# Transformer block with quantized cross-attention and a 16-expert layer: the front reordered, one tile turned by a DMA

## What is computed

```
def fake_quant(x, scale, zp):
    q = clip(round(x / scale + zp), 0, 255)
    return (q - zp) * scale

# 1. attention stage: x [2,512,1024], context [2,1024,1024]
x = x + tanh(g_xattn) * matmul(fake_quant(layernorm(x)), fake_quant(context))

# 2. expert stage on xt = layernorm(x)
logits = xt @ router_w + router_b
scores = softmax(logits) + router_bias
# 2 of 4 groups by their maximum, then 2 of 16 experts in them: gate [1024,16]
for e in range(16):
    h = silu(xt @ w1[e] + b1[e]) * (xt @ w2[e] + b2[e])     # 256 wide
    y = y + gate[:, e] * (h @ w3[e] + b3[e])
z = silu(xt @ sw1 + sb1) * (xt @ sw2 + sb2) @ sw3 + sb3     # shared, 512 wide
x = x + tanh(g_ffn) * (y + z)
```

## Time and profile before

| | us |
|---|---|
| median of 3 runs | 317.7 |
| runs | 317.53 to 319.18 |
| the profiled execution | 317.24 |
| its span in the trace | 315.4 |
| PE busy | 302.6 (96%) |
| DVE busy | 206.3 (65%) |
| ACT busy | 115.0 (36%) |
| POOL busy | 13.9 (4%) |

### The profile page before, as it was taken

One profiled execution on the slowest core, in us unless ns is written; L12 is line 12 of the kernel. 1 busy time (PEld: TensorE's weight loads), 2 busy tenths in 40 slices (PEclk: granted clock), 3 DMA queues, 4 the chain that ended last, 5 costly groups with the idle time before them and its releaser, 6 DMA issues.

```text
span 315.4 us, 4716 instructions
## 1 busy us (share of the span) xinstructions
PE 302.6 (96%) x1867; PEld 153.3 (49%) x1867; DVE 206.3 (65%) x346; ACT 115.0 (36%) x129; POOL 13.9 (4%) x27
## 2 busy tenths in 40 slices
PE   4899899999999999999999999999999999999993
PEld 4653499644444446444444444444444444444441
DVE  3888999999998967776464361748564306135543
ACT  2877689589633559211108000064000000111000
POOL 2100120100002110000000000000000000000000
PEclk9999999999999999999999999999999999999999
DMA  7999908447620547105800008400000000000355
GB/s 234 410 337 321 304 12 250 150 101 214 220 66 0 108 94 72 1 2 167 301 0 2 0 0 290 178 0 0 2 0 0 2 1 1 0 2 0 134 204 202
DMA packets 43543, 34.55 MB, mean 110 GB/s; under 512 B 24060, under 2 KB 38396, under 8 KB 43516
## 3 DMA queue, kind: packets, MB, share of 16 engines
q1 hardware_dynamic: 43508, 34.20, 35.6%
q10 hardware_dynamic: 8, 0.00, 0.0%
HBM read 26.86 MB, written 4.19 MB: 98 GB/s over the span
## 4 chain that ended last, share of the span: by engine, by line
PE 60%; DVE 25%; DMA 4%; ACT 4%; issue 3%; POOL 2%; POOLq 0%; ACTq 0%; DVEq 0%; SPq 0%
PE PS L1426 26%; PE PS L1233 13%; PE PS L1447 13%; PE PS L1274 7%; DVE stats L691 6%; DVE X L778 3%; DVE areaW L755 3%; POOL lnR L399 2%; DMA areaT<-ring 2%; ACT QI L450 1%; DMA ring<-in_L_ffn_sw_dram 1%; DVE S L742 1%; DVE X L1017 1%; DVE area L738 1%; DMA X<-in_x_dram 1%
## 5 line engine op out<-in xcount | busy, mean ns | idle before, releaser
L1233 PE MATMUL PS<-areaT,areaW 128*128 128x512 f16 x288 | 62.5, 379 | 0.0
L1233 PEld LDWEIGHTS PS<-areaT,areaW 128*128 128x128 f16 x288 | 28.0, 98 | 33.7
L1274 PE MATMUL PS<-SW,areaH 128*128 128x512 f16 x192 | 41.8, 379 | 0.0
L1447 PE MATMUL PS<-areaW,areaH 128*128 128x512 f16 x192 | 41.8, 379 | 0.0
L1426 PE MATMUL PS<-areaT,area 128*128 128x512 f16 x192 | 41.6, 379 | 0.0
L1426 PE MATMUL PS<-areaT,areaW 128*128 128x512 f16 x192 | 41.6, 379 | 0.0
L635 ACT ACTIVATE SA<-PS,ecol 128x512 f32<-128x512 f32 x8 | 5.5, 689 | 93.2 <-PE PS L1426 93.2
L1105 DVE SCALAR_TENSOR_TENSOR X<-PS,gcol,X 128x1024 f32<-128x1024 f32 (+1 forms) x18 | 21.0, 1165 | 15.8 <-PE PS L1447 15.8
L1076 DVE SCALAR_TENSOR_TENSOR SA<-PS,ecol,SA 128x512 f32<-128x512 f32 x8 | 6.0, 751 | 38.2 <-ACT SA L635 38.2
L1176 PE MATMUL PS<-area,areaQ 128*128 128x512 f16 x128 | 30.0, 379 | 0.9 <-DVE areaQ L721 0.3
L1274 PEld LDWEIGHTS PS<-SW,areaH 128*128 128x128 f16 x192 | 18.8, 98 | 22.6
(11 more groups left out here) (164 smaller groups left out, 308.8 us busy)
## 6 DMA issues: line engine op xcount, KB each, us to landing
areaT<-in_ctx_dram SPq DMA_DIRECT2D x12, 512.0 KB, 8.1
ring<-in_L_ffn_sw_dram SPq DMA_DIRECT2D x12, 512.0 KB, 5.4
X<-in_x_dram SPq DMA_DIRECT2D x8, 512.0 KB, 5.9
ring<-in_L_ffn_ew_dram SPq DMA_DIRECT2D x4, 1024.0 KB, 7.2
out_dram<-X SPq DMA_DIRECT2D x7, 512.0 KB, 2.6
ring<-in_ctx_dram SPq DMA_DIRECT2D x4, 512.0 KB, 3.8
wrow<-in_L_ffn_ew_dram SPq DMA_DIRECT2D x2, 1024.0 KB, 9.6
rows<-in_L_ffn_eb_dram SPq DMA_DIRECT2D x2, 512.0 KB, 9.5
```

The lines of the kernel that those rows point to most:

```text
L1233: last = mm(PS[:, SU_BANK[half * SC + c] + w, lo:hi], SW[:, wp, 2 * c + w, k, :], XT[:, xp, k, tk], start=(k == 0 and n == 0), stop=(k == ...
L1274: last = mm(PS[:, pb + h, :], HT[:, hp, c, i * P:(i + 1) * P], SW3[:, wp, c, hs], start=(c == 0 and n == 0), stop=(c == SC - 1 and n == 2))
L1447: last = mm(PS[:, 2 * (i % 2) + h, :], HE[:, hp, c, i * P:(i + 1) * P], W3S[j][:, wp, c, hs], start=(c == 0 and n == 0), stop=(c == HC - 1 ...
```

## The change

1. SP loads context tile 0 ahead of x tile 1, x tile 2 ahead of context tile 2, and x tile 3 behind context tile 4.
2. VectorE's and ScalarE's queues of the front are written in another order. All four tiles are copied from PSUM by ScalarE (`evac_q1`). The context column sum is no longer added right behind each clamp, but later where it fits. Four of the six coefficient operations in `cf` now stand behind the first tile's statistics, and a fifth behind tile 0's coefficients.
3. TensorE's order follows; fewer idle products stand in it (14 + 32 + 14 + 30, before 14 + 32 + 14 + 18 + 10 + 26).
4. No `open_block`: the first product into a bank starts it.
5. The fourth normed tile is turned by a transposing transfer that SP issues between weight chunks 6 and 7. TensorE's two transposes and ScalarE's two copies for it are gone. `first_low` runs over the first three tiles (384 columns), then `row_sums`, then all products of the fourth tile.
6. `add_columns` of tiles 5, 6 and 7 runs on GpSimd, each ahead of the tile's attend; tile 4 stays with VectorE.
7. `token_sum` of tiles 6 and 7 and `row_terms(1)` stand behind the second half's coefficients instead of ahead of the fourth `su_gate`; the load of `SB3` stands behind the turned tokens.

The core of the diff:

```diff
@@ SP
+            for r in range(4, 7):
+                load_chunk(r)
+            sp.wait_ge(ln_hi, TB)
+            sp.wait_ge(ln_lo, TB)
+            sp.dma_start_transpose(XT[:, :, :, S - P:S].rearrange("p h k t -> p (h k) t"), WROW[TB - 1]).then_inc(xt3_in, 16)
+            for r in range(7, 10):
                 load_chunk(r)
@@ GpSimd
+            def add_columns(i):
+                nc.gpsimd.tensor_tensor(X[:, i, :], X[:, i, :], RC[:, :], ALU.add).then_inc(col_add, 1)
+
+            pool.wait_ge(rc_rdy, 1)
+            pool.wait_ge(x_int, NT)
             for i in range(TB, NT):
+                if i + 1 < NT:
+                    add_columns(i + 1)
                 rstd(i, 1, 2 * TB + i + 1)
@@ VectorE, second half
             for i in range(TB, NT):
+                if i > TB:
+                    dve.wait_ge(col_add, i - TB)
                 attend(i)
-                add_columns(i)
+                if i == TB:
+                    add_columns(i)
                 bn(i)
                 if i > TB:
                     ln2_lo(i - 1)
                 coefs(i, 1, None, XS, None)
+            token_sum(TB + 2)
+            token_sum(TB + 3)
+            row_terms(1)
             ln2_lo(NT - 1)
@@ TensorE
             def first_high(i, xp, c):
-                pe.wait_ge((tk_hi, tk_lo)[xp], i + 1)
+                if i < TB - 1:
+                    pe.wait_ge((tk_hi, tk_lo)[xp], i + 1)
+                else:
+                    pe.wait_ge(xt3_in, 16)
+                if i == 0 and xp == 0:
+                    pe.wait_ge(at_read, c + 2)
...
-            for i in range(TB):
-                if i == 0:
-                    open_block(0)
+            for i in range(TB - 1):
                 first_high(i, 0, 0)
                 transpose_low(i)
-                if i == 0:
-                    open_block(1)
                 first_high(i, 0, 1)
-                if i < TB - 1:
+                if i < TB - 2:
                     transpose_high(i + 1)
-                else:
-                    row_sums()
                 first_high(i, 1, 0)
                 first_high(i, 1, 1)
-            first_low()
+            for c in range(2):
+                first_low(c, 0, S - P)
+            row_sums()
+            for c in range(2):
+                first_high(TB - 1, 0, c)
+                first_high(TB - 1, 1, c)
+                first_low(c, S - P, S).then_inc(su_done, 1)
```

More of the change, by code:

```diff
@@ L249, in _ @@
             sp.dma_start(sc1[3:4, 0:1], x2_zp.rearrange("(a n) -> a n", a=1)).then_inc(small_in, 16)
+            load_ctx0(0)
             load_x(1)
-            load_ctx0(0)
             load_ctx0(1)
-            load_ctx0(2)
             load_x(2)
+            for k in range(2, 5):
+                load_ctx0(k)
             load_x(3)
-            for k in range(3, KC):
+            for k in range(5, KC):
                 load_ctx0(k)
@@ L301, in _ @@
                 sp.dma_start(CTX1[c], ctx_in[1, c * P:(c + 1) * P, :].rearrange("p (k n) -> p k n", k=4)).then_inc(c1_in[c], 16)
-            for r in range(4, 10):
+            for r in range(4, 7):
[4 more added lines that the diff above has]
+            for r in range(7, 10):
                 load_chunk(r)
@@ L313, in _ @@
                 sp.wait_ge(q1t_in[j], 32)
+            for i in range(TB, NT):
+                turn_tokens(i)
             sp.wait_ge(rs_rdy, TB)
             sp.dma_start(SB3, sb3.partition_broadcast(P)).then_inc(sb3_in, 16)
-            for i in range(TB, NT):
-                turn_tokens(i)
             with nc.allow_non_contiguous_dma(reason="bias vectors laid along the partitions"):
@@ L912, in _ @@
             clamp_x(0)
+            clamp_only(0)
+            dve.wait_ge(x_in[2], 16)
+            bn(2)
+            coefs(1, 1, cf[:, 3:4], None, sc6[:, 1:2])
+            clamp_only(1)
+            dve.wait_ge(sg_T, 1)
+            v.tensor_copy(sc6[:, 4:6], PS[:, 3, 20:22]).then_inc(sc_rdy, 1)
+            coefs(2, 1, cf[:, 3:4], None, sc6[:, 1:2])
+            clamp_only(2)
+            clamp_x(1)
+            add_s2(1)
+            clamp_x(2)
+            dve.wait_ge(x_in[3], 16)
+            bn(3)
+            clamp_only(3)
+            add_s2(2)
+            add_s2(3)
+            coefs(3, 1, cf[:, 3:4], None, sc6[:, 1:2])
+            clamp_only(4)
             link(v.tensor_scalar(cf[:, 8:9], sc6[:, 1:2], -1.0, HALF, ALU.mult, ALU.add))
@@ L1245, in first_high, with first_low @@
                     for k in range(KC):
[L1246 to L1250 removed]
+                        mm(PS[:, 4 + 2 * c + w, tk], SW[:, 0, 2 * c + w, k, :], XT[:, xp, k, tk],
+                           start=(i == 0 and xp == 0 and k == 0), stop=False)
+            def first_low(c, lo, hi):
                 for w in range(2):
[L1252 to L1262 removed]
+                    pe.wait_ge(*lo_done(2 * c + w))
+                    for k in range(KC):
+                        last = mm(PS[:, 4 + 2 * c + w, lo:hi], SW[:, 1, 2 * c + w, k, :], XT[:, 0, k, lo:hi], start=False,
+                                  stop=(hi == S and k == KC - 1))
+                return last
             def shared_down(tile, pb):
@@ L1293, in _ @@
             pe.wait_ge(q1_rdy, 1)
-            for k in range(2):
-                pe.wait_ge(q2_rdy, k + 1)
-                products(0, k)
+            pe.wait_ge(q2_rdy, 1)
+            products(0, 0)
+            idle_products(30)
             transpose_q1(1)
-            idle_products(18)
+            pe.wait_ge(q2_rdy, 2)
+            products(0, 1)
+            pe.wait_ge(q2_rdy, 3)
+            products(0, 2)
+            transpose_q1(2)
             pe.wait_ge(q1_rdy, 2)
@@ L1311, in _ @@
             pe.wait_ge(q1_rdy, 3)
-            for k in range(3):
+            for k in range(4):
                 products(2, k)
             pe.wait_ge(q2_rdy, 5)
-            products(0, 4)
-            products(1, 4)
-            transpose_q1(3)
-            products(2, 3)
-            products(2, 4)
+            for i in range(TB - 1):
+                products(i, 4)
             pe.wait_ge(q2_rdy, 6)
@@ L1322, in _ @@
                 products(i, 5)
+            transpose_q1(3)
             pe.wait_ge(q2_rdy, 7)
-            products(0, 6)
-            products(1, 6)
+            for i in range(TB - 1):
+                products(i, 6)
             pe.wait_ge(q2_rdy, KC)
@@ L1332, in _ @@
             column_sums(1)
-            products(2, KC - 2)
             products(2, KC - 1)
```

109 lines of the change are left out of this document (37 added, 72 removed).

## The result

The changed kernel takes 319.19 us (median of 22 executions, 316.73 to 320.77), the kernel before 317.31 beside it (22 executions, 316.68 to 319.18). The ratio is **1.005, with a 95% interval of 1.0033 to 1.0066**: some 1.6 us slower (1.9 between the two medians), where I had forecast 0.8 us faster. The median is just inside the range of 315.0 to 319.3, but on the other side of no change; 0.14 stood on slower than 319.3. The profiled execution took 319.86, with a span of 318.0 (315.4 before) and a mean granted clock of 0.990 (0.998).

What follows compares the result with a forecast made beforehand. TensorE's products were taken to bound the kernel, the effect showing when it leaves the router. From 317.24 profiled, 0.6 at the column row and 0.2 at the router came off: 316.4, or 316.9 from the 317.7 median; range 315.0 to 319.3.

Steps and rivals of the forecast that it cites:

- the first attends: VectorE's front: tile 0 attended at 28.3 instead of 29.76, tile 1 at 32.7 where it was 32.71.
- TensorE's new waits for VectorE: First half: TensorE idle 1.9 ahead of the first low transposes and 0.9 at tile 2's low part.
- VectorE's wait for the row sums: First half: row sums end at 58.3, row_terms(0) would be reached at 56.3, so VectorE waits 2.0.
- GpSimd's add: Second half: one column add moved to GpSimd takes 2.3, estimated from its select, against 1.22 on VectorE.
- VectorE's first add held back: Second half: VectorE's add to tile 4 waits 1.1 for GpSimd's first add.
- most of TensorE's saving in the first half goes into waits for VectorE: Of 3.8 saved on TensorE, 2.9 goes into new waits, nearly all for VectorE; the first half ends 0.9 earlier.
- the others have 3.2 between a root and the next low part, enough for 2.3: Second half: after tile 4, GpSimd's adds of 2.3 fit before VectorE's next low part, without a wait.
- The third rival: Second half: GpSimd's adds become the bound from 3.5 an add; at 4.5, 319.8 us; chance 0.09.
- I give a fall no chance of its own: TensorE's granted clock: a fall in it got no separate chance in the forecast.
- The later row sums: From 55.8 to 58.3; queues behind 1.8 later; the fourth gate makes TensorE start the column row at 87.95, not 87.66.
- The transposing transfer: Turns the first half's fourth tile, saving TensorE 0.9; takes 6 of 7.2 available, hidden; chance of being late 0.08.
- an earlier first attend is given back: Front: coefs(0) and two more operations ahead of attend(1) leave VectorE only 0.3 earlier from there.

Runs made afterwards that it cites:

- e1_vector_adds: The changed kernel with the three column adds of tiles 5 to 7 back on VectorE; 317.47 us, ratio 1.000 to the kernel before.
- f1_filled: The changed kernel with four products of zeros in the last shared_down tile, filling TensorE's idle time ahead of the router; 316.92 us, ratio 1.0004 to the kernel before.
- f2_hole: The kernel before with two unread sums on VectorE ahead of the first shared_down evacuation, making TensorE idle ahead of the router; ratio 1.0085.
- e4_sums_first: e2_one_input with TensorE's row sums ahead of the low products of three tiles; ratio 0.996 to the kernel before, 0.997 when run again.
- f3_no_turn: e2_one_input with the fourth tile turned by TensorE again, row sums where they stood before, low products of 512 columns; ratio 0.9999 to the kernel before.
- e2_one_input: The changed kernel with lnB of the second norm taking lnA as a per-partition scalar, not a second tensor; 316.55 us, ratio 0.9975 to the kernel before.

## Why the prediction was wrong

*What held.* In the profiled execution: the first attends (28.3 and 32.7 forecast, 28.76 and 33.22 seen), TensorE's new waits for VectorE (1.9 and 0.9; 1.72 and 0.67), VectorE's wait for the row sums (2.0; 1.97), GpSimd's add (2.3; 2.39, 2.35 and 2.34), VectorE's first add held back (1.1 more; 2.06 - 1.22 = 0.84). The claim that most of TensorE's saving in the first half goes into waits for VectorE held: counted from the first attend, the first half is 0.8 longer than before (35.41 against 34.61), so that it ends at 64.17 (64.37 before; I had 63.5).

*The step that failed* is the sentence on GpSimd's adds: "the others have 3.2 between a root and the next low part, enough for 2.3". I had seen one direction of the rule, in the root that waited beside VectorE's subtract, reckoned with the other, and looked for the next two-input operation on VectorE. I took the low part (1024 elements) and passed over lnB, the two-input operation of one element which stands 0.2 behind the root, exactly where GpSimd starts its add. With that price put in (T - 0.4 for each of two tiles, 3.9 at T = 2.35), the sum gives a low part at 119.5 and a landing near 124.3; seen were 119.91 and 124.25. That the landing fits is in part luck: the low part was 0.4 later, and its transfer took 4.28 where I had 4.75. The third rival, GpSimd's adds as the bound, was this case with the wrong threshold: I let it decide from T = 3.5. With T - 0.4 in place of T - 3.2, the landing at 119.3 + (T - 1.2) + 2(T - 0.4) passes 122.25 at T = 1.65, below the 2.3 that I forecast.

*The second* is "I give a fall no chance of its own". I judged the clock by 2.3 us of idle time early in the kernel with the clock at 1.00, and by the front alone. The fall came where TensorE, after an idle 0.75, ran only the router's narrow products. It costs as much again as the delay, 1.28 in the 72 products. In the front, where I looked, a fall does happen (e1_vector_adds) and costs little. The Trainium skill (TensorE: Matmul & The Clock Gate, "Why this matters for your kernels") advises against long idle gaps between bursts of products; here the clock fell behind a gap of 0.75 and one of 1.35 ahead of the router, and f1_filled and f2_hole show it from both sides.

*Terms that were mis-sized, with the mechanism right.* The later row sums: I let them cost 0.3 at the column row, as a wait for the fourth gate. That wait came (0.31), and undoing the lateness brought 0.5 (e4_sums_first). The transposing transfer: I had 0.9 of TensorE's time for the two transposes that it replaces. In f3_no_turn, which has them again, the first half ends 0.44 later than in e2_one_input; at the column row the transfer is worth 0.4 with the sums first (59.76 against 60.14), and nothing without. That an earlier first attend is given back held too: f3_no_turn, without transfer and without later row sums, has the column row 60.14 behind its first attend, where the kernel before has 58.78. Counted from the first attend I had the column row at 87.95 - 28.3 = 59.65, and it came at 60.06. With an attend 0.46 later than forecast on top, nothing was gained there in the profiled execution (88.82, 88.54 before), where I had 0.6.

*Without the two*, the forecast stands: e2_one_input has the ratio 0.9975, where 316.9 over 317.7 was 0.9975. Its column row, though, came 0.6 later behind the first attend than I summed (60.24 against 59.65), and its profiled execution gained nothing (a span of 315.6, 315.4 before), so part of that agreement is an early front in its other executions, or luck; I can't tell the two apart.

## What to carry to other kernels

Before work is put on GpSimd, list every VectorE instruction in its shadow that reads two tensors from SBUF, whatever its size, and give the small ones their factor as a per-partition scalar. When a step makes TensorE idle, as here ahead of a run of narrow products, price the delay and then the clock behind it: idle time that can't be removed may be worth filling with products of zeros. And when a part gains half a microsecond, count its marks from a common event: the start of this kernel varies by more than that.

## What the runs showed of the hardware

- A VectorE scalar_tensor_tensor of [128, 1] with two SBUF inputs, begun 0.25 behind a GpSimd add of [128, 1024], ended with it: 2.11 instead of 0.16. The same product as tensor_scalar with a per-partition scalar took 0.21 beside such an add.
- A GpSimd add of [128, 1024] in float32 takes 2.34 to 2.40; alone it costs the kernel nothing (ratio 0.9998 with the one-input form).
- After an idle 0.75 (1.35 in f2_hole) and then the router's products of 16 and 32 columns, TensorE's granted clock went to 0.50 in the window of 124 and until past 127, and 72 products took 16.84 to 17.04 instead of 15.56. With the gap filled they took 15.58.
- A transposing transfer of one normed tile within SBUF took 7.3 from issue to landing with loads in flight (6.1 to 7.2 in eight other profiled executions), against 4.28 for the last tile's (4.75 in the earlier trace rows), and held SP for 3.61.
- A 512 KB load issued behind four small ones on ScalarE's queue at 2.19 landed at 8.62; issued as SP's fourth, its tile was there by 6.7 to 7.7.
